# Graph network block on one core: batched one-hot comparisons, an fp32 first product, and basis parts placed elsewhere

## The reference

```python
# layer 0: normalised graph convolution, batch norm, exact GELU, residual
xw = x @ W.T
deg = segment_sum(ones, col) ; dinv = rsqrt(deg)       # self loops added
h = segment_sum(dinv[row] * dinv[col] * xw[row], col) + b
h = gelu((h - mean) * rsqrt(var + eps) * gamma + beta)
x = layernorm(x + h + x)
# layer 1: two relational layers with 2 relations and 30 bases
w = einsum('rb,bio->rio', att, basis)                  # basis: 30 x 512 x 512
gate = sigmoid(x @ gate_w[r])
agg = segment_sum(where(type == r, (gate * x)[col] @ w[r]), row)
h1 = relu(agg + x @ root1 + bias1) ; out = the same with the second weights
x = layernorm(x + out)
```

## Time and profile before

| quantity | value |
|---|---|
| median of 3 runs | 326.71 us |
| profiled execution | 326.88 us |
| its span | 325.0 us |
| mean granted TensorE clock | 0.942 of full speed |
| PE busy | 283.5 us (87%) |
| DVE busy | 175.3 us (54%) |
| ACT busy | 135.3 us (42%) |
| DMA | 73.68 MB, mean 227 GB/s |

### The profile page before, as it was taken

The page is one execution under the profiler, slowest core; times in us unless marked ns, Lnnn a source line. Parts: engine busy times, 40 slices in busy tenths (PEclk is TensorE's granted clock), DMA queues, the critical chain, the costliest instruction groups (busy, mean ns, idle before and its releaser), DMA issues.

```text
span 325.0 us, 4963 instructions
## 1 busy us (share of the span) xinstructions
PE 283.5 (87%) x1711; PEld 193.4 (60%) x1711; DVE 175.3 (54%) x538; ACT 135.3 (42%) x265; POOL 36.5 (11%) x71
## 2 busy tenths in 40 slices
PE   1768899885969999568999999999997999999991
PEld 1653455432336786424767656647795777787771
DVE  3878787999967847686310132233325125433333
ACT  4596868899701368647243114111313142100000
POOL 1001000000002900551000000000003600010000
PEclk9987999998695999779999999999998999999997
DMA  6974869599997999739998677975001400001112
GB/s 175 335 327 158 336 257 356 207 388 416 352 385 282 314 354 418 313 103 367 382 381 318 260 292 303 418 294 246 2 0 32 132 0 0 2 0 33 33 34 63
DMA packets 12759, 73.68 MB, mean 227 GB/s; under 512 B 1952, under 2 KB 2195, under 8 KB 4540
## 3 DMA queue, kind: packets, MB, share of 16 engines
q1 hardware_dynamic: 11282, 70.82, 57.4%
q0 software_dynamic: 1104, 2.36, 2.8%
q10 hardware_dynamic: 346, 0.17, 0.3%
HBM read 72.05 MB, written 1.28 MB: 226 GB/s over the span
## 4 chain that ended last, share of the span: by engine, by line
PE 61%; DVE 22%; issue 7%; DMA 4%; DVEq 2%; ACT 1%; POOL 1%; ACTq 0%; POOLq 0%
PE psW L495 13%; PE psM L476 10%; PE psM L477 9%; PE psM L478 9%; PE psM L717 6%; PE psM L737 6%; DVE oh_key L1047 4%; DMA basis_ring<-in_L_gnn_basis_dram 3%; PE psM L623 3%; DVE B L1038 2%; PE psE L570 2%; DVEq L1032 2%; DVE w L1027 1%; DVE x_sum L1170 1%; DVE AT L1103 1%
## 5 line engine op out<-in xcount | busy, mean ns | idle before, releaser
L495 PE MATMUL psW<-basis_ring,S 128*32 128x512 f32 x512 | 68.2, 651 | 3.2 <-DMA basis_ring<-in_L_gnn_basis_dram 3.1
L1217 DVE SCALAR_TENSOR_TENSOR zg<-psM,gate,zg 125x512 fp32r<-125x512 f32 x20 | 15.0, 751 | 59.5 <-ACT zg L891 59.5
L1047 DVE TENSOR_SCALAR oh_key<-iota_f,key 128x160 f16<-128x160 f16 x162 | 36.0, 262 | 2.6 <-PE psE L570 1.4
L785 ACT ACTIVATE oh_diff<-iota_f,edgeT 128x128 f16<-128x128 f16 x108 | 34.1, 389 | 3.4 <-DVEq L964 3.4
L495 PEld LDWEIGHTS psW<-basis_ring,S 128*32 128x32 f32 x512 | 13.9, 115 | 32.5 <-issue 26.4
L476 PE MATMUL psM<-w,hlT 128*125 128x512 f32 x80 | 33.1, 414 | 0.1
L891 ACT ACTIVATE zg<-psM,gate 125x512 fp32r<-125x512 f32 x20 | 13.8, 688 | 46.1 <-PE psM L478 45.7
L477 PE MATMUL psM<-w,hlT 128*125 128x512 f32 x80 | 32.3, 404 | 0.0
L478 PE MATMUL psM<-w,hlT 128*125 128x512 f32 x80 | 32.1, 402 | 0.0
L570 PEld LDWEIGHTS psE<-oh_key,oh_src 128*125 128x125 f16 x162 | 16.0, 150 | 25.2 <-issue 19.2
L570 PE MATMUL psE<-oh_key,oh_src 128*125 128x160 f16 x162 | 21.3, 261 | 10.2 <-issue 6.6
(11 more groups left out here) (159 smaller groups left out, 430.5 us busy)
## 6 DMA issues: line engine op xcount, KB each, us to landing
basis_ring<-in_L_gnn_basis_dram SPq DMA_DIRECT2D x64, 1024.0 KB, 7.1
root_raw<-in_L_gnn_root_dram POOLq DMA_DIRECT2D x32, 64.0 KB, 3.6
xs<-in_x_dram SPq DMA_DIRECT2D x1, 1120.0 KB
out_dram<-xs SPq DMA_DIRECT2D x5, 224.0 KB
w_raw<-in_L_gnn_W_dram SPq DMA_DIRECT2D x1, 1024.0 KB, 10.9
bias_b<-in_L_gnn_bias_dram POOLq DMA_DIRECT2D x1, 250.0 KB, 3.8
xs<-in_x_dram SPq DMA_DIRECT2D x1, 130.0 KB
out_dram<-xs SPq DMA_DIRECT2D x5, 26.0 KB
```

The source lines that it names most:

```text
L495: m = nc.tensor.matmul(psW[32 * j:32 * j + 32, cc % 2, :], S[:, cc % 2, cc // CH, q].rearrange("p k r -> p (k r)"), ring[:, n % RING, j, : ...
L785: nc.scalar.activation(oh_diff[:, g % 3, j * P:(j + 1) * P], iota_f[:, 0:P], ACT.Abs, bias=edgeT[:, 0, g * G + j:g * G + j + 1], scale=-1. ...
L1047: v.tensor_scalar(oh_key[:, t % OH, :], iota_f[:, 0:KEYS], key[:, t:t + 1], None, ALU.is_equal) \
```

## The change

- **One-hot blocks.** `places` and `oh_diff` go, so ScalarE makes none of them. `key` and the places are copied once as pairs (`key_pairs`, `place_pairs`, fp16). Per group VectorE makes all six `oh_src` blocks (126 wide) with one two-source comparison and all six `oh_key` blocks with a second one (`one_hots`). The register reads of the two windows of a group stand behind the first and the second comparison (`window_at`), and both windows are added one behind the other. PE waits once per group.
- **First product.** ScalarE copies each turned block as fp32 (`turned_out`), `turned_low` goes, and each of the 20 steps is one fp32 product instead of three fp32r ones. W0's rows are loaded permuted, in four DMAs, so the product comes out in the other order of columns and one of two turned copies of the vectors goes.
- **Steps and parts.** Two `xw` steps and one basis pair per three groups; 16 parts lie in the loop where 24 lay, five `xw` steps and 48 parts behind it.
- **Middle.** The identity is put into `B` by ScalarE before the loop, and taken out of `BB` later; the diagonal blocks are made by POOL; their products stand behind the first `agg0` step and ScalarE copies them; `w_merge`, `w_low`, `w_high` and `w_first` of blocks 1 to 3 stand elsewhere.

```diff
-OH = 12
-GA = 4
+OH = 3 * G
+PLACES = PC + PC % 2
...
-        FIRST_XW = 4
+        PARTS_IN = 15
-        TURNED_LOW_AT = {1: (0, 1), 2: (2, 3), 3: (4, 5), 4: (6, 7), 5: (8,)}
-        FIRST_AT = {8: 0, 17: 1}
-        HIGH_AT = {13: 0, 22: 1}
-        MERGE_AT = {11: 0, 20: 1}
-        LOW_AT = {14: 0, 23: 1}
+        MERGE_AT = {16: 0}
+        LOW_AT = {19: 0}
...
+            pool.wait_ge(dinv_ready, 1)
+            for c in range(NC):
+                nc.gpsimd.tensor_scalar(diag[:, c, :], ident[0:PC, 0:PC], dinv_p[:, c:c + 1], None, ALU.mult) \
+                    .then_inc(diag_ready, 1)
...
-                mm3(bank(("xw", c))[0:PC, :], xT_hi[:, k, n], xT_lo[:, k, n], w0T_hi[:, k], w0T_lo[:, k],
-                    k == 0, k == KC - 1)
+                last[0] = nc.tensor.matmul(bank(("xw", c))[0:PC, :], xT[:, k, n], w0T[:, k], start=(k == 0), stop=(k == KC - 1))
...
-                basis_upto(9 * g // 10)
+                xw_upto(2 * (g - 3) // 3)
+                basis_upto(min(2 * g // 3 - 2, PARTS_IN))
...
-            basis_upto(24)
-            basis_upto(25)
-            basis_upto(26)
+            basis_upto(17)
+            basis_upto(19)
...
-                basis_upto((28, 30, 31, 32)[f])
-            basis_upto(33)
+                basis_upto((21, 23, 25, 27)[f])
...
+            basis_upto(29)
-                basis_upto((35, 36, 37)[c])
+                basis_upto((31, 33, 35)[c])
-                    basis_upto(39 + KC * h + f)
+                    basis_upto((37, 37, 39, 39, 41, 41, 43, 43)[KC * h + f])
-                            basis_upto(47 + 7 * (R * c + r) // 5)
+                            basis_upto((45, 47, 47, 49, 51, 51, 53, 55, 55, 57)[R * c + r])
-                    basis_upto(min(60 + KC * h + f, 2 * CH * SUB - 1))
+                    basis_upto((57, 59, 59, 61, 61, 63, 63, 63)[KC * h + f])
...
-                if f == 2:
+                if f == 1:
+                    w_high(1)
+                if f == KC:
                     w_high(2)
                     w_first(3)
...
+            def one_hots(out, pairs, first, n, width):
+                pair = iota_f[:, 0:width].rearrange("p (k i) -> p k i", i=2)
+                shape = [P, n, width // 2, 2]
+                return v.tensor_tensor(out, pair.unsqueeze(1).broadcast_to(shape),
+                                       pairs[:, first:first + n].unsqueeze(2).broadcast_to(shape), ALU.is_equal)
+
+            for g in range(NG):
+                if g >= 3:
+                    dve.wait_ge(adj_used, G * (g - 2))
+                src = oh_src[:, g % 3].rearrange("p (t e) -> p t e", t=G)[:, :, 0:PLACES]
+                one_hots(src.rearrange("p t (k i) -> p t k i", i=2), place_pairs, g * G, G, PLACES)
+                at = [window_at(2 * (g - 2))] if g >= 2 else []
+                one_hots(oh_key[:, g * G % OH:g * G % OH + G].rearrange("p t (k i) -> p t k i", i=2), key_pairs, g * G, G, KEYS) \
+                    .then_inc(key_ready, 1)
+                if g >= 2:
+                    at.append(window_at(2 * (g - 2) + 1))
...
-                link(v.tensor_tensor(AT[:, c], B[:, c, 0, 0:N2], B[:, c, 1, 0:N2], ALU.add))
-                d = AT[:, c, c * PC:(c + 1) * PC]
-                v.tensor_tensor(d, d.bitcast(F32), ident[0:PC, 0:PC], ALU.add).then_inc(at_ready, 1)
-            w_merge(2)
+                v.tensor_tensor(AT[:, c], B[:, c, 0, 0:N2], B[:, c, 1, 0:N2], ALU.add).then_inc(at_ready, 1)
...
+            w_merge(1)
+            dve.wait_ge(dinv_b_ready, 2)
...
-                if c == 1:
-                    w_merge(3)
...
-            w_low(3)
+            w_low(2)
+            w_merge(3)
```

More of the change, by code:

```diff
@@ L264, in gnn_block @@
                 use(("agg0", f, h), "dve")
+                if (f, h) == (0, 0):
+                    for i in range(2):
+                        use(("dinv", i), "act")
                 for b in BB_STEPS[2 * f + h]:
@@ L559, in _, with xw_upto @@
             done()
+            steps_done = [0]
+            def xw_upto(n):
+                for i in range(steps_done[0], n):
+                    xw_part(i)
+                steps_done[0] = max(steps_done[0], n)
             for i in range(FIRST_TURNS):
@@ L626, in _ @@
                     done()
+                    if (f, h) == (0, 0):
+                        pe.wait_ge(diag_ready, NC)
+                        for i, (c0, c1) in enumerate(((0, 4), (4, NC))):
+                            wait_free(pe, ("dinv", i))
+                            for c in range(c0, c1):
+                                last[0] = nc.tensor.matmul(bank(("dinv", i))[:, (c - c0) * PC:(c - c0 + 1) * PC],
+                                                           ones_f[0:PC, :], diag[:, c, :], start=True, stop=True)
+                            done()
                     for b in BB_STEPS[2 * f + h]:
@@ L816, in _, with xw_out @@
-            w_first(2)
+                to, ps = turned_from(i)
+                nc.scalar.activation(to, ps, ACT.Copy).then_inc(free_act, 1)
+                act.wait_ge(free_act, releaser[:uses[turned[i]] + 1].count("act"))
+                act.sem_inc(in_turned, 1)
+            def xw_out(c):
+                wait_full(act, ("xw", c))
+                release(nc.scalar.activation(xw[:, c, :], bank(("xw", c))[0:PC, :], ACT.Copy), ("xw", c), "act")
+            for i in range(len(turned)):
+                turned_out(i)
@@ L977, in _ @@
             link(v.tensor_tensor(key[:], key[:], edgeT[:, 2, :], ALU.add))
+            link(v.tensor_copy(key_pairs[:], key[:].unsqueeze(2).broadcast_to([P, T, 2])))
             def build_S():
@@ L1058, in _ @@
[L1058 to L1063 removed]
+                    dve.wait_ge(b_zero, NC)
+                for i, w in enumerate(range(2 * (g - 2), 2 * (g - 1)) if g >= 2 else ()):
+                    add_window(w, at[i])
+                if g == ROUNDS_AT:
+                    rounds()
@@ L1112, in _ @@
             for c in range(NC):
-                last = v.tensor_scalar(diag[:, c, :], ident[0:PC, 0:PC], dinv_p[:, c:c + 1], None, ALU.mult)
-            last.then_inc(diag_ready, 1)
-            for c in range(NC):
                 dve.wait_ge(z_hi, c + 1)
@@ L1229, in z_parts @@
                             .then_inc(root_ready, 1)
+            for d in range(NC):
+                own_edge = BB[:, d * (R * NC + 1) * PC:(d * (R * NC + 1) + 1) * PC]
+                last = v.tensor_tensor(own_edge, own_edge.bitcast(F32), ident[0:PC, 0:PC], ALU.subtract)
+            link(last)
             z_parts(0)
```

184 lines of the change are left out of this document (70 added, 114 removed).

## The result

| | before | after |
|---|---|---|
| median | 326.86 us (326.15 to 328.33) | 323.6 us (321.52 to 325.44, 4 runs) |
| ratio | | 0.989, 95% interval 0.9849 to 0.9931 |
| profiled execution, span | 326.88, 325.0 us | 324.19, 322.2 us |
| last window starts | 93.97 us | 77.70 us |
| first `agg0` product | 107.22 | 91.22 |

A forecast was written before the change was run, and what follows sets the result against it. PE was taken to bound nearly everything but the edge loop, whose new groups fill VectorE and PE equally. Terms -19.3 + 0 + 1.6 + 2.5 + 1.9 = -13.3 from 326.88 gave 313.5 us, range 305 to 324.

The forecast's parts named there:

- Comparisons: Edge loop, VectorE: two two-source fp16 comparisons per group at half the fp32 per-element price, 0.47 + 0.57 = 1.04 us.
- rival 1: Edge loop: fp16 comparisons cost as much as fp32 ones, group 2.65 us, 6.0 lost behind the loop, 333.4 us; chance 0.07.
- rival 2: Edge loop: PE's low clock sets the pace, 325 us if for a third of it, 317 for a tenth; strong form 0.09.
- Group 1.9 us: Edge loop: VectorE needs 1.9 us a group, comparisons, windows and 0.2 for register reads included; range 1.75 to 2.65.
- forecast of 75.0 us: End of the edge loop: 22.7 + 43.7 + 5.5 + 3.1 = 75.0 us against 94.30, a gain of 19.3 us.
- xw step 0.85: PE: one first-product step takes 0.85 us; five late ones (4.3 us) run beside the adjacency's additions and cost nothing.
- To the first aggregation, 0: From the loop to the first aggregation step: -1.3 us at full PE clock, +3 at the low one, taken as 0.
- Last GELU +1.6: ScalarE: a high and a first part ahead of the last GELU outlast a gap of 1.81 us, costing 1.6 us.
- Transfers: Edge loop: one pair of parts per 5.7 us needs 368 GB/s, near the edge of the 368 and 424 seen.
- Norm and turning, root1 at T + 19.2: Between the turning back of h (T) and root1: four pairs instead of two, root1 at T + 19.2 instead of 16.7, +2.5 us.
- First-layer sums +1.9: Sums of the first layer, behind root1: three pairs of parts instead of two on a full PE, +1.9 us.
- Rival 3: Ring brings only 330 GB/s: 5.6 us lost in the loop, about 4 in the middle, 323 us; chance 0.10.

The follow-up runs named there:

- no_pairs: The changed kernel with keys and places broadcast as single fp16 elements instead of copies in pairs; 338.07 us, ratio 1.0261 to the kernel before.
- light_after: The changed kernel with only half the bytes of every basis part but the first four loaded; 315.07 us, ratio 0.9611 to the kernel before.
- old_parts: The changed kernel with basis parts and weight steps where the kernel before had them (24 parts in the loop); 317.27 us, ratio 0.9677 to the kernel before.

## Why the prediction was wrong

The direction was right, the size was not: 13.2 us forecast, 3.3 measured. The step that failed is the aggregation, for which the sum had no term for waits on the ring. Point by point:

- **Comparisons** (1.04 us from the half slope; 0.55 and 0.66, with 0.08 to 0.1 of each under the next instruction): right. The table of the Trainium skill that the prediction names (VectorE: DVE Perf Modes, "The perf-mode tier table") lists bf16 and not fp16; the trace has the double rate for fp16, 0.55 us against the 0.94 of no_pairs. **Full price** (rival 1): excluded, and no_pairs shows what it would have been. Its group is 2.62 us; the rival's terms add up to 2.63, not to the 2.65 written there. The time is 338.07 us against my 333.4, since what lies behind the last window grew by 10.4 us there, not by 6.0. **PE's clock in the loop** (rival 2): 0.97 from 22 to 78 us; no.
- **Group 1.9 us**: mis-sized, 1.98. I took reads behind the comparisons for nearly free. They cost 0.26 us a group against reads directly ahead. The forecast of 75.0 us is for the end of the last window, which ends at 78.0: 23 x 0.08 = 1.8 of these 3.0 us; the rest is not itemised. With the reads ahead it ends at 73.2 us, earlier than my 75.0.
- **xw step 0.85**: 0.91. The five late ones take 4.56 us, from 78.30, and the adjacency's additions run from 79.29 to 82.98 beside them, so the cover held.
- **To the first aggregation, 0**: 77.70 to 91.22 is 13.5 us, before 107.22 - 93.97 = 13.25. Right in sum.
- **Last GELU +1.6**: right; ScalarE's own two pieces hold it back by 1.4 us.
- **The aggregation: no term of its own beside the GELU's.** From the first `agg0` product to T it was 25.8 us and is 32.7: 5.3 us more than the GELU's 1.6. This is the step that failed. Under "Transfers" I weighed the loop alone and found it "near the edge but not over it", and I put no wait for parts here. Of the growth of 6.9 us, 3.1 are the waits of 1.10 and 2.02 us for the ring, 1.5 the slow products behind the second (113.50 to 118.77 against 124.94 to 128.68 before), 1.4 the GELU, and about 1.0 the `diag` products that moved in. light_after, with half the bytes, has 27.8 us here. The loop drew only 279 GB/s, not 368: at 1.98 us a group, a pair per three groups would be 353, and VectorE's extras stretch the eight pairs (27.98 to 76.45 us) to one every 6.9 us, 303. The transfers that it no longer carries come due in stretches that follow: one pair more directly ahead of the aggregation, two more ahead of root1. And the aggregation already ran at 1.03 of its DMA engines before, so a ring that was used up at its start could not catch up. That the two pairs directly ahead use it up is read from the timeline; no kernel with only these moved was run.
- **Norm and turning, root1 at T + 19.2**: mis-sized by 1.6 us; it is at T + 20.8, with waits of 1.10, 2.14 and 1.60 us for the ring. I had priced the landing at 400 GB/s; the stretch carried 315.
- **First-layer sums +1.9**: 2.2 for all that lies behind root1. Right.
- **Rival 3** gave the right time, 323, and the right heading, transfers; I gave it 0.10. The number was luck. It had 5.6 us in the loop and 4 in the middle, where the loop lost none and the middle ten. Its condition, a ring at 330 GB/s, held from 95 to 110 us (319) but not before or after (414 from 110 to 119). What it lacked is that the ring was idle for 0.28 of the loop and full afterwards.

So the gain is real on VectorE and in the loop, and it was paid back by the place of the parts. old_parts and light_after show it from two sides: the one leaves the transfers in the loop, the other halves them.

## What to carry to other kernels

Where a stream must be loaded anyway, count its bytes per stage against what the stage behind already carries, and ask how full the ring is when a busy stretch begins. Here work that left a stage took its transfers along, and the stretch at a DMA share of 1.0 paid for them in waits, though its engines had the time. Look also at whether a register read stands behind a wait on its engine's queue: in this loop two of them needed 1.3 us where 1.12 us of work was queued, and one on either side of the wait was hidden.

## What the runs showed of the hardware

- A register read for VectorE (TENSOR_LOAD and what belongs to it) occupies its sequencer for 0.6 to 0.7 us, also where the engine shows only 0.17 us of idle.
- A two-source fp16 comparison of 756 elements takes 0.55 us where the repeated operand has two addresses innermost, and 0.94 where it is one element; 960 elements take 0.65 and 1.15.
- One fp32 product of a 128x125 block with 512 columns takes 0.91 us, against 0.71 for the three fp32r products that it replaced, both at a granted clock of 1.00.
- After a wait of 2.02 us PE took 2.66 us for ten products that take 1.73 otherwise, at a granted clock of 0.59 from 113.5 to 116 us; after one of 1.10 us it took 1.75. light_after, without those waits, was granted 1.00 there.
- DMA engines that are busy all the time do not always carry the same: in after 319 GB/s from 95 to 110 us (share 1.02) and 414 from 110 to 119 (1.01); in the kernel before 301 and 316 GB/s in the two stretches from 107 to 119 us (0.97 and 1.04), and 419 from 119 to 125 (1.01). In both kernels the low rate stands where the aggregation begins; why was not tested.
